# Half of the pair products of a feature-interaction kernel with the batch on the partitions

## The chip, the cores and the metric

The kernel runs on one core of a Trainium2 chip. The metric is the device time of one execution in microseconds, lower is better. On the core, TensorE multiplies matrices into PSUM, VectorE and ScalarE work on elements, GpSimd here only issues gathers, and SyncE only issues loads.

## The reference

A recommendation model's top: 32 embedding tables are looked up for a batch of 1,024, every pair of the 32 fields gets a bilinear form with a 64 x 64 matrix of its own, and three dense layers follow. All is fp32.

```python
iu, ju = jnp.triu_indices(32, k=1)                       # 496 pairs
p, q = e[:, iu, :], e[:, ju, :]                          # e: 1024 x 32 x 64, gathered
z = jnp.einsum('bpe,fpe,bpf->bp', p, kernel, q)          # kernel: 64 x 496 x 64
h = jnp.concatenate([z, dense_ctx], axis=1)              # 1024 x 512
h = jnp.maximum(h @ W_top1 + b_top1, 0.0)                # 512 -> 512
h = jnp.maximum(h @ W_top2 + b_top2, 0.0)                # 512 -> 256
y = h @ W_top3                                           # 256 -> 1
```

## The kernel before

The batch is cut into four quarters of 256 (`QB`). Two fields of 64 features make a **pack** of 128 partitions, so a quarter has 16 packs. GpSimd gathers the rows of a pack with four indirect DMAs into `raw`, batch on the partitions (L173). TensorE transposes the pack into the PSUM bank `prep_ps` (L307), and ScalarE copies it to `xt`, features on the partitions (L192). SyncE loads the pair matrices of pack k into `k_sb` (L161).

The pairs of pack k with the packs m below it are done in **units** (`UNITS`, L23) of up to two m each, 64 units in a quarter. For a unit TensorE multiplies the stationary pair matrices `k_sb` with the moving `xt` of pack m, four matmuls of 64 x 128 by 256 columns (L289 and L290, on the two halves of the array at a time), into one slot of `t_ps`. A unit with a single m (`len(ms) == 1`) uses the free quarter of the slot for the pairs inside the packs (L295, L297). `t_ps` has three slots (`TRING`), taken in the order of `TURNS`; before a slot is taken again TensorE waits for `prod_done`, the multiply that read it (`take_turn`, L268). VectorE multiplies the slot by `xt` of pack k into `prod` (L252; a single-m unit takes three instructions, L256, L258, L260). Now the 64 products of a pair lie on partitions, and TensorE sums them: a matmul with the stationary 0/1 matrix `sel_sb` of 32 columns adds the partitions into a row of `z_ps` (L321, L324), four such matmuls at a time on the four column groups.

The order is written out by hand. Four units make a **burst**. In burst b TensorE transforms the four units, then runs a piece of the layers of the quarter before, where one is due, then transposes packs that the next burst needs, then sums the products of burst b - 1 (L366 to L377). The layers have four **pieces** per quarter (L333), each of which takes a slot of `t_ps` in turn: two of 16 instructions with `w1_sb` (L343), one with `w2_sb` (L352), and one of four (L358). ScalarE copies `z_ps` to `zt` (L199) and applies the layers' bias and ReLU (L209, L212). Every fp32 matmul is two instructions in the trace.

Of the kernel before, what the change touches and what calls it, by code (L numbers as in the profile page):

```python
# [11 lines left out]
PACKS = FIELDS // 2  # L12
W = 2 * QB
ZT = 2
RAW = 16
XRING = 2 * PACKS
TRING = 3
PRING = 8
BURST = 4

UNITS = [(k, tuple(range(m, min(m + 2, k)))) for k in range(1, PACKS) for m in range(0, k, 2)]  # L23
NU = len(UNITS)
NB = NU // BURST
TILE_BURSTS = NB // ZT
PACK_COL = [P * (k * (k - 1) // 2) + EMBED * (k // 2) for k in range(PACKS + 1)]
KCOLS = PACK_COL[PACKS]


def weight_cols(k, m):

    begin = PACK_COL[k] + P * m
    return slice(begin, begin + (EMBED if m == k else P))


def burst_sums(b):

    sums = [(u, n) for u in range(b * BURST, (b + 1) * BURST) for n in range(2)]
    return sorted(sums, key=lambda un: un[1] == 1 and len(UNITS[un[0]][1]) == 1)  # L40

Z_SLOT = {un: (b // TILE_BURSTS, at % 4, 2 * (b % TILE_BURSTS) + at // 4)
          for b in range(NB) for at, un in enumerate(burst_sums(b))}

FREE = [Z_SLOT[u, 1] for u, (_, ms) in enumerate(UNITS) if len(ms) == 1]
FREE_GROUPS = sorted({(t, g) for t, g, _ in FREE})


def packs_due(b):

    q, at = divmod(b, NB)
    if q >= QUARTERS:
        return []
    last = UNITS[at * BURST + BURST - 1][0]
    due = [k for k in range(PACKS) if k <= last and (at == 0 or k > UNITS[at * BURST - 1][0])]
    if at == 0 and q:
        due = due[2:]
    due = [q * PACKS + k for k in due]  # L60
    if at == NB - 1 and q < QUARTERS - 1:
        due += [(q + 1) * PACKS, (q + 1) * PACKS + 1]
    return due


def before_sums(b):


    return packs_due(b)[:1] if b > NB else []


def after_sums(b):
    return packs_due(b)[len(before_sums(b)):]

PIECES = 4
PIECE_BURST = 2
# [4 lines left out]
def piece_after(b):  # L83

    q, at = divmod(b, NB)
    return (q - 1, at - PIECE_BURST) if q and 0 <= at - PIECE_BURST < PIECES else None

# [5 lines left out]

def turns():

    out = []
    for b in range(QUARTERS * NB):
        out += [("unit", b * BURST + n) for n in range(BURST)]
        if piece_after(b):
            out.append(("piece", piece_after(b)))  # L100
    return out + [("piece", (QUARTERS - 1, piece)) for piece in range(PIECES)]

# [5 lines left out]
def build(nc, ids, tables, kmat, dense, w1, b1, w2, b2, w3, sel, sel_dense, ident, y):  # L108
    fp32, i32 = mybir.dt.float32, mybir.dt.int32
    ALU, ACT = mybir.AluOpType, mybir.ActivationFunctionType  # L110
    ctx = ExitStack()
    with ctx:
# [9 lines left out]
        sel_dense_sb = sb("sel_dense_sb", [P, len(FREE_GROUPS), 32])  # L122
        w1_sb = sb("w1_sb", [P, 2 * ZT, H1])
# [4 lines left out]
        dense_sb = sb("dense_sb", [P, BATCH])  # L128
        k_sb = sb("k_sb", [P, KCOLS])
        raw = sb("raw", [P, RAW, BT, 2, EMBED])  # L130
        xt = sb("xt", [P, XRING, QB])
        prod = sb("prod", [P, PRING, 4, QB])
        zt = sb("zt", [P, ZT, W])
        h1 = sb("h1", [P, H1 // P, QB])
        h2 = sb("h2", [P, H2 // P, QB])
        y_sb = sb("y_sb", [1, BATCH])

        t_ps = ctx.enter_context(nc.psum_tensor("t_ps", [P, TRING, 4, QB], fp32))
        prep_ps = ctx.enter_context(nc.psum_tensor("prep_ps", [P, QB], fp32))
# [309 lines left out]
```

## Time and profile before

| | us |
|---|---|
| median of 3 runs | 472.48 |
| lowest, highest | 471.53, 472.54 |
| the profiled execution | 471.08 |
| span of its profile | 469.3 |
| TensorE busy (share of the span) | 438.2 (93%) |
| VectorE busy | 305.6 (65%) |
| GpSimd busy | 241.9 (52%) |
| ScalarE busy | 42.0 (9%) |
| mean granted TensorE clock | 0.996 |

The busy time of an engine is the union of its instructions' records. Matmuls overlap in the array, so the mean duration of one is longer than the distance from one to the next. The granted clock is at its full level in nearly every stretch. "Idle before" names what an engine waited for. The chain of work that ended last follows each wait back to what ended it.

### The profile page before, as it was taken

The page shows a single profiled execution, that of the slowest core. Times are in us where ns is not written, and L with a number is a line of the kernel's source. Part 1 is how long each engine was busy: PE and PEld are TensorE (multiplying, and loading weights), DVE is VectorE, ACT ScalarE, POOL GpSimd, SP SyncE. Part 2 cuts the span into 40 slices and gives each one's busy share as a digit, 9 for nine tenths or more (in the row PEclk, how much of TensorE's full clock was granted, in tenths as well). Part 3 has the DMA queues.
Part 4 walks back from the last instruction along what each step waited for, and adds up shares of the span by engine and source line. Part 5 has one row for each costly group of instructions (what it writes and reads, how often), then busy time and mean ns, then how long its engine had stood idle before and what let it go on. Part 6 is the DMA issues. An engine that isn't in the chain of part 4 may idle for free.

```text
span 469.3 us, 7916 instructions
## 1 busy us (share of the span) xinstructions
PE 438.2 (93%) x3432; PEld 263.1 (56%) x3432; DVE 305.6 (65%) x320; ACT 42.0 (9%) x101; POOL 241.9 (52%) x260
## 2 busy tenths in 40 slices
PE   0159999999999999999999999999999999999988
PEld 0036556556456765665556674565556765565646
DVE  0045878788774656788777456788787437878850
ACT  1000000100111110000011110000001110000002
POOL 5777777777777777777777777753300000000000
PEclk9998999999999999999999999999999999999999
DMA  4444454511111111111111111110000000000000
GB/s 125 110 114 135 134 168 154 162 28 27 27 27 28 27 27 29 27 26 30 27 30 25 27 29 27 27 22 13 11 3 0 1 1 0 1 1 1 0 1 0
DMA packets 11834, 19.41 MB, mean 41 GB/s; under 512 B 5141, under 2 KB 5785, under 8 KB 11673
## 3 DMA queue, kind: packets, MB, share of 16 engines
q0 software_dynamic: 8192, 8.40, 10.1%
q1 hardware_dynamic: 2592, 8.34, 5.6%
q10 hardware_dynamic: 1016, 2.17, 1.3%
q8 instruction: 27, 0.44, 0.4%
q14 instruction: 7, 0.05, 0.0%
HBM read 18.89 MB, written 0.00 MB: 40 GB/s over the span
## 4 chain that ended last, share of the span: by engine, by line
PE 91%; POOL 5%; issue 2%; DMA 1%; DVE 1%; ACT 0%; DVEq 0%
PE t_ps L289 46%; PE z_ps L321 23%; PE t_ps L343 6%; POOL raw L173 5%; PE prep_ps L307 4%; PE t_ps L295 3%; PE t_ps L352 3%; PE t_ps L290 1%; PE z_ps L324 1%; PE t_ps L358 1%; DVE prod L252 1%; DMA raw<-tbl,ids_sb 1%; PE z_ps L329 1%; DMA ids_sb<-ids 1%; ACT xt L192 0%
## 5 line engine op out<-in xcount | busy, mean ns | idle before, releaser
L252 DVE TENSOR_TENSOR prod<-t_ps,xt 128x1024 f32<-128x1024 f32 x224 | 259.1, 1215 | 93.1 <-PE t_ps L290 93.1
L173 POOL DMA_INDIRECT raw<-tbl,ids_sb x256 | 241.7, 944 | 93.7 <-issue 76.2
L289 PE MATMUL t_ps<-xt,k_sb 64*128 64x256 f32 x960 | 232.4, 390 | 0.0
L290 PE MATMUL t_ps<-xt,k_sb 64*128 64x256 f32 x960 | 232.4, 390 | 0.0
L289 PEld LDWEIGHTS t_ps<-xt,k_sb 64*128 64x128 f32 x960 | 172.3, 188 | 67.7 <-issue 26.6
L290 PEld LDWEIGHTS t_ps<-xt,k_sb 64*128 64x128 f32 x960 | 172.4, 189 | 0.0
L321 PE MATMUL z_ps<-prod,sel_sb 128*32 128x512 f32 x960 | 122.9, 599 | 0.5 <-DVE prod L260 0.5
L321 PEld LDWEIGHTS z_ps<-prod,sel_sb 128*32 128x32 f32 x960 | 26.3, 109 | 54.7 <-issue 46.5
L256 DVE TENSOR_TENSOR prod<-t_ps,xt 128x512 f32<-128x512 f32 x32 | 21.9, 685 | 53.2 <-PE t_ps L297 53.2
L307 PE MATMUL prep_ps<-ident_sb,raw 128*128 128x128 f32 x128 | 28.5, 305 | 27.8 <-DMA raw<-tbl,ids_sb 26.7
L192 ACT ACTIVATE xt<-prep_ps 128x256 f32<-128x256 f32 x64 | 24.5, 382 | 284.6 <-PE prep_ps L307 283.3
L307 PEld LDWEIGHTS prep_ps<-ident_sb,raw 128*128 128x128 f32 x128 | 13.9, 144 | 55.1 <-issue 35.9
L343 PE MATMUL t_ps<-zt,w_sb 128*128 128x256 f32 x128 | 29.5, 385 | 0.8 <-ACT zt L199 0.8
L343 PEld LDWEIGHTS t_ps<-zt,w_sb 128*128 128x128 f32 x128 | 23.8, 190 | 6.6 <-DVE prod L252 2.4
L295 PE MATMUL t_ps<-xt,k_sb 64*64 64x256 f32 x64 | 21.1, 410 | 0.0
L297 PE MATMUL t_ps<-xt,k_sb 64*64 64x256 f32 x64 | 21.0, 410 | 0.0
L324 PE MATMUL z_ps<-prod,sel_sb 128*32 128x256 f32 x64 | 16.7, 379 | 0.0
L352 PE MATMUL t_ps<-h,w_sb 128*128 128x256 f32 x64 | 14.8, 384 | 0.0
L258 DVE TENSOR_TENSOR prod<-t_ps,xt 64x256 f32<-64x256 f32 x32 | 13.7, 427 | 0.4
L260 DVE TENSOR_TENSOR prod<-t_ps,xt 64x256 f32<-64x256 f32 x32 | 13.3, 417 | 0.4
L352 PEld LDWEIGHTS t_ps<-h,w_sb 128*128 128x128 f32 x64 | 11.9, 190 | 2.6 <-DVE prod L252 1.1
L209 ACT ACTIVATE h<-t_ps,b_sb 128x256 f32<-128x256 f32 x16 | 7.6, 473 | 57.2 <-PE t_ps L343 57.2
(15 smaller groups left out, 42.0 us busy)
## 6 DMA issues: line engine op xcount, KB each, us to landing
raw<-tbl,ids_sb POOLq DMA_INDIRECT x256, 2.5
w_sb<-w ACTq DMA_DIRECT2D x1, 1024.0 KB
k_sb<-kmat SPq DMA_DIRECT2D x1, 992.0 KB, 5.0
k_sb<-kmat SPq DMA_DIRECT2D x1, 896.0 KB
k_sb<-kmat SPq DMA_DIRECT2D x1, 864.0 KB, 4.5
k_sb<-kmat SPq DMA_DIRECT2D x1, 768.0 KB, 4.2
k_sb<-kmat SPq DMA_DIRECT2D x1, 736.0 KB, 4.0
k_sb<-kmat SPq DMA_DIRECT2D x1, 640.0 KB, 3.9
```

The lines of the kernel that those rows point to most:

```text
L173: nc.gpsimd.indirect_dma_start(raw[:, p % RAW, t, f, :], None, tables[2 * k + f], bass.IndirectOffsetOnAxis(ap=ids_sb[:, q * BT + t, 2 * k ...
L192: nc.scalar.activation(xt[:, p % XRING, :], prep_ps[:], ACT.Copy).then_inc(x_copied, 1)
L252: nc.vector.tensor_tensor(prod[:, own], t_ps[:, slot], xt[:, here:here + 1, :].broadcast_to([P, 4, QB]), ALU.mult).then_inc(prod_done, 1)
L256: nc.vector.tensor_tensor(prod[:, own, 0:4:2, :], t_ps[:, slot, 0:4:2, :], xt[:, here:here + 1, :].broadcast_to([P, 2, QB]), ALU.mult)
L289: nc.tensor.matmul(t_ps[:, slot, i, :], k_sb[0:EMBED, cols], xt[0:EMBED, x, :], start=True, stop=True)
L290: last = nc.tensor.matmul(t_ps[:, slot, 2 + i, :], k_sb[EMBED:P, cols], xt[EMBED:P, x, :], start=True, stop=True)
L295: nc.tensor.matmul(t_ps[EMBED:P, slot, 1, :], k_sb[0:EMBED, cols], xt[0:EMBED, xa, :], start=True, stop=True)
L307: last = nc.tensor.transpose(prep_ps[:, t * P:(t + 1) * P], raw[:, p % RAW, t, :, :], ident_sb[:])
L321: last = nc.tensor.matmul(z_ps[rows, :], weights, prod[:, own, 2 * n:2 * n + 2, :], start=(pos == 0), stop=(pos == 15 and (tile, group) no ...
L324: last = nc.tensor.matmul(z_ps[rows, 0:QB], weights, prod[:, own, 2, :], start=False, stop=False)
L343: last = nc.tensor.matmul(t_ps[:, slot, 2 * n, :], w1_sb[:, t, m * P:(m + 1) * P], zt[:, t // 2, t % 2 * QB:(t % 2 + 1) * QB], start=(t == ...
L352: last = nc.tensor.matmul(t_ps[:, slot, 2 * n, :], w2_sb[:, t, n * P:(n + 1) * P], h1[:, t, :], start=(t == 0), stop=(t == H1 // P - 1))
```

## The change

Half of the work changes its layout. For 16 blocks in a quarter (`BATCH_GROUPS`: pack k of 4 to 15 with the packs 0 to 3, and pack k of 12 to 15 also with the packs 4 to 7), the stationary operand is now `xt` of pack k for 128 samples, and the pair matrices `k_sb` move, 512 columns a matmul. The result in `t_ps` has the batch on the partitions. VectorE multiplies it by `raw`, the gathered rows themselves, into `prod_a` or `prod_d`, and the 64 products of a pair are now neighbours on one partition. Of these **batch units**, 32 in a quarter and 128 in all, VectorE sums every third and the last six itself with one reduction each (47), and ScalarE the other 81, each with 16 activations of 64 elements that also write their sum to `zb`. The other 32 units of a quarter, the **feature units**, stay as they were, column sums on TensorE included; their sums fill one `z_ps` bank per quarter instead of two.

A **round** now has four feature units and the four batch units of the round before, alternating (`order()`); there are 8 rounds in a quarter. The column sums come once per round. `t_ps` keeps its three slots. Once per quarter TensorE transposes `zb` (`turn_sums`), and ScalarE copies it to `zbt`, which feeds half of the first layer. Packs are transposed and copied in pairs of 512 columns. `raw` and `xt` have 24 slots (`SLOTS`); a gather into a slot that batch units read waits for the last batch unit of that quarter.

The core of the diff; what is left out are the constants' arithmetic, the placing of weights on the host, and the names of columns.

```diff
+GROUP = 4
+GF = 2 * GROUP
 W = 2 * QB
-RAW = 16
-XRING = 2 * PACKS
+SLOTS = 24
 TRING = 3
-PRING = 8
+FRING = 8
+ARING = 6
+DRING = 2
+BATCH_GROUPS = {k: (() if k < GROUP else (0,) if k < 3 * GROUP else (0, 1)) for k in range(PACKS)}
+F_UNITS = [(k, tuple(range(m, min(m + 2, k)))) for k in range(1, PACKS)
+           for m in range(0, k, 2) if m // GROUP not in BATCH_GROUPS[k]]
+B_UNITS = [(k, j, t) for k in range(PACKS) for j in BATCH_GROUPS[k] for t in range(BT)]
...
+def order():
+    out = []
+    for r in range(LAST + 1):
+        q, at = divmod(r, ROUNDS)
+        feature = [("F", q, at * BURST + n) for n in range(BURST)] if r < LAST else []
+        q, at = divmod(r - 1, ROUNDS)
+        batch = [("B", q, at * BURST + n) for n in range(BURST)] if r else []
+        mixed = [x for n in range(BURST) for x in feature[n:n + 1] + batch[n:n + 1]]
+        out.append(mixed)
+    return out
...
+def on_vector(q, u):
+    n = q * NBU + u
+    return n % 3 == 0 or n >= QUARTERS * NBU - 6
...
 # GpSimd
-                if p >= RAW:
-                    pool.wait_ge(transposed, p - RAW + 1)
+                if p >= SLOTS:
+                    before_q, before_k = divmod(p - SLOTS, PACKS)
+                    pool.wait_ge(prep_done, pair_copied(before_q, before_k))
+                    if before_k < 2 * GROUP:
+                        pool.wait_ge(prod_done, COUNT["B", before_q, NBU - 1])
...
 # ScalarE
+            def sum_along(q, u):
+                own = SCALAR_UNITS.index((q, u)) % ARING
+                act.wait_ge(prod_done, COUNT["B", q, u])
...
+                for n in range(2):
+                    for f in range(GF):
+                        last = nc.scalar.activation(prod_a[:, own, n, f, :], prod_a[:, own, n, f, :], ACT.Copy,
+                                                    accum_out=zb[:, q % 2, t, col + n * GF + f:col + n * GF + f + 1])
+                last.then_inc(reduced_a, 1)
...
+            for r in range(LAST + 1):
+                if piece_after(r):
+                    copy_layer(*piece_after(r))
+                if turned_after(r) is not None:
+                    copy_turned(turned_after(r))
+                for j in before_sums(r + 1):
+                    copy_pair(j)
+                if r and r % ROUNDS == 0:
+                    copy_z(r // ROUNDS - 1)
+                for j in after_sums(r + 1):
+                    copy_pair(j)
...
+                for kind, q, u in ORDER[r]:
+                    if kind == "B" and not on_vector(q, u):
+                        sum_along(q, u)
...
 # VectorE
+            def batch_multiply(q, u):
...
+                dve.wait_ge(t_done, COUNT["B", q, u])
+                nc.vector.tensor_tensor(
+                    out.rearrange("p n (g c) f -> p n g (c f)", g=GROUP),
+                    t_ps[:, slot].rearrange("p (n h) (g w) -> p n (h g) w", n=2, w=2 * EMBED),
+                    raw[:, first:first + GROUP, t, :].unsqueeze(1).broadcast_to([P, 2, GROUP, 2 * EMBED]),
+                    ALU.mult).then_inc(prod_done, 1)
+            def sum_along(q, u):
...
+                nc.vector.tensor_reduce(zb[:, q % 2, t, col:col + 2 * GF],
+                                        prod_d[:, n % DRING].rearrange("p n c f -> p (n c) f"),
+                                        AX.X, ALU.add).then_inc(reduced_d, 1)
...
 # TensorE
+            def batch_transform(q, u):
+                k, j, t = B_UNITS[u]
+                slot = take_turn(TURN_OF["B", q, u])
...
+                nc.tensor.matmul(t_ps[:, slot, 0:2, :], xt[0:EMBED, x, t * P:(t + 1) * P], k_sb[0:EMBED, cols],
+                                 start=True, stop=True)
+                nc.tensor.matmul(t_ps[:, slot, 2:4, :], xt[EMBED:P, x, t * P:(t + 1) * P], k_sb[EMBED:P, cols],
+                                 start=True, stop=True).then_inc(t_done, 1)
...
+            def turn_sums(q):
+                pe.wait_ge(prep_copied, PREP_COUNT["turn", q] - 1)
+                pe.wait_ge(reduced_a, sum(x[0] <= q for x in SCALAR_UNITS))
+                pe.wait_ge(reduced_d, sum(x[0] <= q for x in VECTOR_UNITS))
+                for c in range(2):
+                    for t in range(BT):
+                        at = c * QB + t * P
+                        last = nc.tensor.transpose(prep_ps[:, at:at + P], zb[:, q % 2, t, c * P:(c + 1) * P], ident_sb[:])
+                last.then_inc(prep_done, 1)
```

On TensorE, around the sums of a burst in the first quarter, the kernel before has sums (L321, L324), a transpose of one pack (L307) and then unit after unit, each with its wait for a slot (`prod_done`):

```order
L321 MATMUL z_ps<-prod,sel_sb 32x512 [waits z_copied,prod_done]
L321 MATMUL z_ps<-prod,sel_sb 32x512 x6
L324 MATMUL z_ps<-prod,sel_sb 32x256
L307 MATMUL prep_ps<-ident_sb,raw 128x128 [waits x_copied,gathered13]
L307 MATMUL prep_ps<-ident_sb,raw 128x128
L289 MATMUL t_ps<-xt,k_sb 128x256 [waits prod_done]
L290 MATMUL t_ps<-xt,k_sb 128x256
L289 MATMUL t_ps<-xt,k_sb 128x256
L290 MATMUL t_ps<-xt,k_sb 128x256
```

In the changed kernel, in the second quarter, a batch unit (L455, L457) follows every feature unit, and a pair of packs (L469) is transposed between two blocks of units, where `gathered` and `prep_copied` are waited for:

```order
L455 MATMUL t_ps<-k_sb,xt 128x512 [waits prep_copied,prod_done]
L457 MATMUL t_ps<-k_sb,xt 128x512
L469 MATMUL prep_ps<-ident_sb,raw 128x128 [waits gathered0,prep_copied]
L469 MATMUL prep_ps<-ident_sb,raw 128x128
L469 MATMUL prep_ps<-ident_sb,raw 128x128 [waits gathered1]
L469 MATMUL prep_ps<-ident_sb,raw 128x128
L493 MATMUL z_ps<-prod,sel_sb 32x512 [waits z_copied,prod_done]
L493 MATMUL z_ps<-prod,sel_sb 32x512 x5
L496 MATMUL z_ps<-prod,sel_sb 32x256 x2
L437 MATMUL t_ps<-xt,k_sb 128x256 [waits prep_copied,prod_done]
L438 MATMUL t_ps<-xt,k_sb 128x256
```

Between two blocks of sums there are now eight units, each with a wait for a slot, instead of four.

On VectorE the kernel before has only the multiplies, here a stretch with one single-m unit:

```order
L252 TENSOR_TENSOR prod<-t_ps,xt 128x1024 [waits t_done,summed,x_copied]
L252 TENSOR_TENSOR prod<-t_ps,xt 128x1024 [waits t_done]
L252 TENSOR_TENSOR prod<-t_ps,xt 128x1024 [waits t_done,x_copied]
L252 TENSOR_TENSOR prod<-t_ps,xt 128x1024 [waits t_done]
L256 TENSOR_TENSOR prod<-t_ps,xt 128x2x256 [waits t_done,summed]
```

The changed one alternates feature (L359, L363) and batch multiplies (L385), with a reduction (L399) one unit behind every third batch unit:

```order
L385 TENSOR_TENSOR prod_a<-t_ps,raw 128x1024 [waits t_done,reduced_a]
L359 TENSOR_TENSOR prod<-t_ps,xt 128x1024 [waits t_done,prep_copied]
L385 TENSOR_TENSOR prod_d<-t_ps,raw 128x1024 [waits t_done,reduced_d]
L359 TENSOR_TENSOR prod<-t_ps,xt 128x1024 [waits t_done,prep_copied]
L399 TENSOR_REDUCE zb<-prod_d 128x16 [waits prod_done]
L385 TENSOR_TENSOR prod_a<-t_ps,raw 128x1024 [waits t_done,reduced_a]
L359 TENSOR_TENSOR prod<-t_ps,xt 128x1024 [waits t_done,summed,prep_copied]
```

The reductions stand in the one queue that also frees the slots of `t_ps`.

On ScalarE the copies of the packs and of the layers stood alone before; now the sums of a round's batch units stand between one round's copies and the next round's, as here in the second quarter:

```order
L270 ACTIVATE xt<-prep_ps 128x512 [waits prod_done,prep_done]
L296 ACTIVATE prod_a,zb<-prod_a 128x64 [waits prod_done]
L296 ACTIVATE prod_a,zb<-prod_a 128x64 x15
L296 ACTIVATE prod_a,zb<-prod_a 128x64 [waits prod_done]
L296 ACTIVATE prod_a,zb<-prod_a 128x64 x15
L296 ACTIVATE prod_a,zb<-prod_a 128x64 [waits prod_done]
L296 ACTIVATE prod_a,zb<-prod_a 128x64 x15
L311 ACTIVATE h<-t_ps,b_sb 128x256 [waits layer_done] x2
L270 ACTIVATE xt<-prep_ps 128x512 [waits prod_done,prep_done]
```

A copy that is due while such sums run waits for them, since the queue is in order.

## Rows read from the trace of the kernel before

**Rows 1.** The page: busy us (share) xinstructions, and the chain that ended last

```profile
PE 438.2 (93%) x3432; PEld 263.1 (56%) x3432; DVE 305.6 (65%) x320; ACT 42.0 (9%) x101; POOL 241.9 (52%) x260
...
PE 91%; POOL 5%; issue 2%; DMA 1%; DVE 1%; ACT 0%; DVEq 0%
```

**Rows 2.** The page's costliest groups: busy us, mean ns | idle before, releaser

```profile
L252 DVE TENSOR_TENSOR prod<-t_ps,xt 128x1024 f32<-128x1024 f32 x224 | 259.1, 1215 | 93.1 <-PE t_ps L290 93.1
...
L307 PEld LDWEIGHTS prep_ps<-ident_sb,raw 128*128 128x128 f32 x128 | 13.9, 144 | 55.1 <-issue 35.9
```

**Rows 3.** The timeline of TensorE, 300 to 316 us: start us, us, what

```profile
301.01 0.44 PE L307 MATMUL prep_ps<-ident_sb,raw 128*128 128x128 f32 x2
301.38 1.92 PE L321 MATMUL z_ps<-prod,sel_sb 128*32 128x512 f32 x16
303.13 0.60 PE L329 MATMUL z_ps<-dense_sb,sel_dense_sb 128*32 128x256 f32 x4
303.66 0.48 PE L289 MATMUL t_ps<-xt,k_sb 64*128 64x256 f32 x1
...
304.20 0.38 PE L289 MATMUL t_ps<-xt,k_sb 64*128 64x256 f32 x1
...
304.42 0.38 PE L289 MATMUL t_ps<-xt,k_sb 64*128 64x256 f32 x1
...
309.53 0.48 PE L289 MATMUL t_ps<-xt,k_sb 64*128 64x256 f32 x1
```

**Rows 4.** The timeline of VectorE in the same stretch

```profile
301.86 0.68 DVE L256 TENSOR_TENSOR prod<-t_ps,xt 128x512 f32<-128x512 f32 x1
302.56 0.43 DVE L258 TENSOR_TENSOR prod<-t_ps,xt 64x256 f32<-64x256 f32 x1
303.00 0.42 DVE L260 TENSOR_TENSOR prod<-t_ps,xt 64x256 f32<-64x256 f32 x1
304.94 4.62 DVE L252 TENSOR_TENSOR prod<-t_ps,xt 128x1024 f32<-128x1024 f32 x4 [1.53 <-PE t_ps L290]
310.79 4.62 DVE L252 TENSOR_TENSOR prod<-t_ps,xt 128x1024 f32<-128x1024 f32 x4 [1.23 <-PE t_ps L290]
```

**Rows 5.** The chain in order of time: start us, us, what; quarters and pieces

```profile
128.75 0.41 PE t_ps L289
...
194.96 0.43 PE z_ps L329 x4
...
253.89 3.72 PE t_ps L343 x16
...
263.48 3.65 PE t_ps L343 x16
...
303.30 0.43 PE z_ps L329 x4
```

**Rows 6.** The timeline of the start: transposes of packs 2 and 3, a gather, the first unit

```profile
19.61 0.69 PE L307 MATMUL prep_ps<-ident_sb,raw 128*128 128x128 f32 x2 [4.20 <-DMA raw<-tbl,ids_sb]
...
24.72 0.94 POOL L173 DMA_INDIRECT raw<-tbl,ids_sb  x1 [0.30 <-issue]
...
24.80 0.69 PE L307 MATMUL prep_ps<-ident_sb,raw 128*128 128x128 f32 x2 [4.51 <-DMA raw<-tbl,ids_sb]
25.42 0.28 PEld L289 LDWEIGHTS t_ps<-xt,k_sb 64*128 64x128 f32 x1 [0.33 <-issue]
```

**Rows 7.** The timeline of the end: the first layer of the last quarter

```profile
455.58 7.15 PE L343 MATMUL t_ps<-zt,w_sb 128*128 128x256 f32 x32 [0.82 <-ACT zt L199]
```

**Rows 8.** The groups of ScalarE's copies, shapes kept apart

```profile
L192 ACT ACTIVATE xt<-prep_ps 128x256 f32<-128x256 f32 x64 | 24.5, 382 | 284.6 <-PE prep_ps L307 283.3 <-ACT y_sb L215 1.3
...
L199 ACT ACTIVATE zt<-z_ps 128x512 f32<-128x512 f32 x8 | 4.8, 597 | 36.6 <-PE z_ps L329 36.6
```

More of the change, by code:

```diff
@@ L37, in burst_sums @@
[L37 to L54, printed above, removed]
-        return []
[L56 to L63, printed above, removed]
@@ new lines, with pairs_due @@
+ORDER = order()
+COUNT = {unit: n + 1 for n, unit in enumerate(x for units in ORDER for x in units)}
+QUARTER_DONE = [max(COUNT["F", q, NF - 1], COUNT["B", q, NBU - 1]) for q in range(QUARTERS)]
+def on_vector(q, u):
+    n = q * NBU + u
+    return n % 3 == 0 or n >= QUARTERS * NBU - 6
+VECTOR_UNITS = [(q, u) for q in range(QUARTERS) for u in range(NBU) if on_vector(q, u)]
+SCALAR_UNITS = [(q, u) for q in range(QUARTERS) for u in range(NBU) if not on_vector(q, u)]
+def pairs_due(r):
+    q, at = divmod(r, ROUNDS)
+    if r >= LAST:
+        return []
+    last = F_UNITS[at * BURST + BURST - 1][0] // 2
+    first = F_UNITS[at * BURST - 1][0] // 2 + 1 if at else 0
+    return [q * PACKS // 2 + j for j in range(first, last + 1)]
@@ L94, in turns @@
+PREP_COUNT = {use: n + 1 for n, use in enumerate(prep_uses())}
 def turns():
     out = []
[L97 to L101, printed above, removed]
+    for r, units in enumerate(ORDER):
+        out += units
+        if piece_after(r):
+            out.append(("piece",) + piece_after(r))
+    return out + [("piece", QUARTERS - 1, piece) for piece in range(PIECES)]
@@ L156, in _ @@
             for k in range(1, PACKS):
[L157 to L159 removed]
+                if k >= GROUP:
+                    sp.wait_ge(prep_done, PREP_COUNT["pair", (k - GROUP) // 2])
                 cols = slice(PACK_COL[k], PACK_COL[k + 1])
@@ L320, in feature_sums @@
-                    if n == 0 or len(UNITS[u][1]) == 2:
+                    own = u % FRING
+                    if n == 0 or len(F_UNITS[u][1]) == 2:
                         last = nc.tensor.matmul(z_ps[rows, :], weights, prod[:, own, 2 * n:2 * n + 2, :],
-                                                start=(pos == 0), stop=(pos == 15 and (tile, group) not in FREE_GROUPS))
+                                                start=(pos == 0), stop=(pos == 15 and group not in FREE_GROUPS))
                     else:
-                        last = nc.tensor.matmul(z_ps[rows, 0:QB], weights, prod[:, own, 2, :],
-                                                start=False, stop=False)
@@ L326, in feature_sums @@
-                if at % TILE_BURSTS == TILE_BURSTS - 1:
-                    for n, (tile, group) in enumerate(FREE_GROUPS):
-                        if tile == at // TILE_BURSTS:
-                            last = nc.tensor.matmul(z_ps[32 * group:32 * group + 32, QB:W], sel_dense_sb[:, n, :],
-                                                    dense_sb[:, q * QB:(q + 1) * QB], start=False, stop=True)
+                        last = nc.tensor.matmul(z_ps[rows, 0:QB], weights, prod[:, own, 2, :], start=False, stop=False)
@@ L331, in feature_sums @@
+                if at == ROUNDS - 1:
+                    for n, group in enumerate(FREE_GROUPS):
+                        last = nc.tensor.matmul(z_ps[32 * group:32 * group + 32, QB:W], sel_dense_sb[:, q, n, :],
+                                                dense_sb[:], start=False, stop=True)
                 last.then_inc(summed, 1)
             def layer(q, piece):
-                slot = take_turn(TURN_OF["piece", (q, piece)])
+                slot = take_turn(TURN_OF["piece", q, piece])
```

352 lines of the change are left out of this document (218 added, 134 removed).

## The prediction

> **What bounds the kernel now.** I read the page's busy times and chain first. TensorE is on 91% of the chain that ended last and VectorE on 1% [rows 1]: almost everything between start and end is TensorE's instruction stream. Then the groups of instructions: VectorE's big multiply ran 224 times and was idle 93.1 us before it, every time for a matmul into `t_ps` [rows 2]; VectorE waits for TensorE, not the other way round. Then the timeline of one burst, to see what the stream consists of. A pair of matmuls on the two halves of the array starts every 0.215 us, a unit is four such pairs, 0.86 us; a full burst is 303.66 to 309.53 [rows 3]. Sixteen sum instructions take 1.75 us (301.38 to 303.13), two transposes 0.37, and each change of tile shape about 0.1. VectorE needs 4.62 us for four full units, 1.135 each when queued ((4.62 - 1.215) / 3), and then idles 1.2 to 1.5 us [rows 4]. So in a burst of 5.5 to 5.9 us VectorE has only about 1.2 us of air. That small air is what the change must live from.
>
> **What it removes.** Half of the units lose their two column-sum matmuls. Sums happen once per round of eight units, 32 times instead of 64. One such block costs TensorE 1.75 + 0.1 to enter it and 0.2 to leave it, about 2.1 us: 32 x 2.1 = 67 us less TensorE work. The transforms do not get cheaper: a batch unit moves 2 x 512 columns where a feature unit moves 4 x 256, in the same pairs, 0.86 us by [rows 3]. Four transposes per quarter are added, 0.65 + 0.1 us, 3 us in all. On TensorE's work alone the kernel would fall to about 405.
>
> **What it adds.** VectorE keeps one multiplication per unit (the batch one reads 1,024 elements of PSUM and writes 1,024; I take 1.135, the row it is nearest to) and gets 47 reductions. No reduction is in the trace. It reads 1,024 elements of a partition: an upper bound is a lone 1.215 us, a lower one 0.68, the 512-element row [rows 2, 4]; I take 1.135, since it reads as many elements as the multiply. VectorE: 305.6 + 47 x 1.135 = 359 us. ScalarE gets 81 units of 16 activations, 1,296 of them, each with an accumulator output.
>
> **Why the freed time does not reach the end.** `t_ps` still has three slots, so TensorE's unit n waits for VectorE's unit n - 3. In a burst of four units that never bites. In a round of eight it does. Take a round from TensorE's first unit at 0. VectorE starts 1.28 later (303.66 to 304.94) [rows 3, 4]. TensorE's eighth unit needs VectorE's fifth done: five multiplies 5.68, plus on average two thirds of a reduction 0.76, plus 0.43 for each `len(ms) == 1` unit (0.70 + 0.44 + 0.43 against 1.135, [rows 4]), 0.32 on average, plus 0.13 for the end of the record and the semaphore: 8.17. Its own 0.86 makes 9.03. Then four transposes (0.37 for two, 0.14 for each more, the time of its weight load: 0.65) [rows 2, 3], 0.1, the sums 1.75, 0.1: a plain round is 11.6 us. The bursts it replaces take 2 x 5.5 to 5.9. A piece of the layers adds 3.7 (a burst with one lasts 263.48 - 253.89 = 9.6, without 5.9 [rows 5]) and waits for the sixth unit's slot, 0.6: 15.9. A quarter is three such, one with the short last piece 13.4, one with the turned sums 12.4, three plain, and 1.4 for the second of two pairs that wait for the one `prep_ps` bank: 109.7 us. Before, a quarter is 303.30 - 194.96 = 108.3 [rows 5]. The steady state gains nothing: what the sums gave back is spent waiting for slots. With half as many rounds, the sums, transposes and pieces form stretches of 2.6 to 6.9 us in which VectorE is fed from at most three slots.
>
> **Start.** Packs land every 5.0 us (19.61, 24.80) [rows 6]. The old kernel works from 25.4 on one pack at a time, and its second quarter begins at 128.75 [rows 5, 6]. In the new one TensorE does round 0 (four units) and then, in its own order, transposes packs 4 to 7 before anything of round 1, so round 1 begins when pack 7 has landed and is copied: 24.8 + 4 x 5.0 + 1.2 = 46. Seven rounds of 11.6 and two waits for a copy put round 8, the second quarter, at 129: only half a microsecond later, because in the old kernel, too, the first quarter goes by what GpSimd gathers. Gathers of later quarters now wait for the last batch unit of the quarter before; GpSimd needs 1.25 us each [rows 6], 10 us for the eight of a pair of packs, and a round is 11.6, so they stay just hidden.
>
> **End.** The last four batch units have no feature unit beside them and their sums lie on VectorE: 1.28 + four multiplies and five reductions, 10.2, then transposes and copy 1.4, then the layers, 455.58 to 469.3 = 13.7 [rows 7]: 26.6 us from the start of the last round. Sum with ScalarE free: 129 + 3 x 109.7 + 26.6 = 485, that is +16 on the span of 469.3, of which 4 are the quarters' and 11 the end's (128.75 + 3 x 108.3 leaves the old one 15.6).
>
> **ScalarE.** Let a be what one accumulating activation takes when queued. Rows give 0.382 us for 256 columns and 0.597 for 512 [rows 8]: 0.84 ns a column and 0.167 fixed, so 0.221 for 64. The program that is built has a second ScalarE instruction behind each of them, which writes the accumulator. Low end: both overlap by the 0.08 that VectorE's rows show (1.215 against 1.135) and the second costs one fixed part: 0.221 + 0.167 - 0.16 = 0.23; were the second free, 0.14. High end: no overlap, 0.39. ScalarE is in program order: copy of the pair, then the two or three batch units of the round, then the next copy, for which TensorE waits. Three units need 48a + 0.9. At a = 0.23 that is 11.9, a few tenths more than a plain round; at 0.28 it is 14.3, 2.7 late, in some 13 plain rounds of three units, 35 us, of which the rounds without a due pair (about a third) hide their part: +24 us. I take 0.28: an instruction without a tensor to read should cost less than a whole fixed part, but ScalarE need not overlap as VectorE does. Beyond 0.31 ScalarE sets the time: 47 until its first unit, 1,296a, 37 of its other work, 13 of waits at 32 copies, 20 at the end: 0.33 gives 545, 0.39 gives 622.
>
> The Trainium skill's page "ScalarE: Activation LUTs", section "What ACT_TABLE_LOAD costs", gives 186 ns + 0.833 ns a column with 93 ns of overlap: an estimate of 0.15 us for 64 columns, accumulator not counted; by it ScalarE would never be late and the sum would stay 485. It agrees with the trace's 0.382 within 17 ns for a lone one; the overlap no row here shows. The skill's page "VectorE: DVE Perf Modes", section "The TRN2 errata", speaks against this change: an SBUF source costs ScalarE 224 cycles fixed against 172 from PSUM, paid per instruction, and it advises tiles of 512 elements or more. By it 64 columns are an estimate of 0.24 us before any accumulator read, and the sum rises to 490 or more. No run here shows an SBUF source on ScalarE.
>
> **Rivals.** (1) ScalarE keeps up (a at most 0.24): 485 to 495. For it: 0.23 is a bound from rows. (2) ScalarE becomes the bound (a above 0.31): 530 to 600. For it: nothing in the trace shows ScalarE instructions overlapping. (3) Faster: slots do not hold TensorE. That needs the batch multiply and the reduction clearly under the 1.135 row; then VectorE keeps ahead, and the time is 469.3 - 67 + 3 + 16 of start and end = 421. The two rows of VectorE at 1,024 and 512 elements scale with elements, which speaks against it; it breaks even only if both cost about 1.0 us. (4) The middle case, my forecast: ScalarE late in the rounds with three units, 497 to 528.
>
> **How the numbers follow.** Span 485 + 24 = 509; the profiled execution took 471.08 with a span of 469.3, so 1.8 lies outside, and the median of the runs is 1.4 above it: 512. Chances: forecast 0.40, keeps up 0.28, ScalarE the bound 0.21, faster 0.09, no difference 0.02. Range: 484, the foot of rival 1, to 585, which is a = 0.36; a tenth stays below, a tenth above. A measurement of this kernel tells about 0.2% from no change, so faster 0.09, same 0.02, slower 0.89.
>
> **What would show it.** In the profile after: busy TensorE near 380 us with idle time before `t_ps` matmuls whose releaser is VectorE or a ScalarE copy (right), or TensorE still above 90% of the chain (rival 3). First sums at 55 to 56 us. Sums of column type every 11.6 us in rounds without pieces and 15 to 16 with them. The activation of L296 with its accumulator instruction: 16 of them per unit in 3.7 us is rival 1, 4.5 the forecast, over 5 rival 2, and then ScalarE leads the chain. Reduction near 1.2 us; a batch multiply longer than 1.3 would add to every round. The prediction is wrong if rounds are shorter than 11 us while `t_ps` has three slots.

## The result, and the profile after

The changed kernel takes 494.68 us (median of 4 runs, 493.90 to 495.66) where the kernel before takes 472.0: a ratio of 1.0485, 95% interval 1.0455 to 1.0516. Slower, inside the range, and 17 us under the predicted 512. It is the case that the prediction called rival 1, ScalarE keeps up (485 to 495). The profiled execution took 494.39 with a span of 492.6.

The page after, busy times and chain, answers to [rows 1]:

```profile
PE 409.6 (83%) x2416; PEld 196.9 (40%) x2416; DVE 355.8 (72%) x367; ACT 346.4 (70%) x2661; POOL 241.9 (49%) x260
...
PE 38%; issue 20%; DVE 19%; ACT 10%; POOL 9%; DMA 2%; DVEq 0%; ACTq 0%; POOLq 0%
```

TensorE fell from 91% of the chain to 38%, VectorE rose from 1% to 19%. Most of "issue" is VectorE too: of the chain's 98.5 us under that name, 73 stand right before an instruction of VectorE, for instance between its back-to-back instructions from 285.9 to 290.5 us. Together that is a third of the span. No engine is over 83% busy: the time is now made of engines that wait for each other. The page's groups (line, engine, operation, busy us, mean ns, idle before them) say what the new instructions cost, beside [rows 2]:

```profile
L296 ACT ACTIVATE prod_a<-prod_a 128x64 f32<-128x64 f32 x1296 | 309.4, 243 | 2.2 <-ACT y_sb L317 1.2
L296 ACT ACTIVATION_READ_ACCUMULATOR prod_a<-prod_a 128x1 f32 x1296 | 245.3, 189 | 0.0
...
L359 DVE TENSOR_TENSOR prod<-t_ps,xt 128x1024 f32<-128x1024 f32 x96 | 116.3, 1212 | 41.2 <-PE t_ps L438 39.5
...
L385 DVE TENSOR_TENSOR prod_a<-t_ps,raw 128x1024 f32<-128x1024 f32 x81 | 97.9, 1209 | 0.0
...
L399 DVE TENSOR_REDUCE zb<-prod_d 128x16 f32<-128x1024 f32 x47 | 56.5, 1204 | 0.0
```

The batch multiply (1.209) and the reduction (1.204) cost what the old multiply did (1.215). Who waits for whom is in the waits (us in total, times, longest); lines 437 and 455 are the first transforms of a feature and a batch unit, 385 the batch multiply:

```profile
PEld t_ps L437 <- DVE prod_a L385: 61.3, 48, 2.0
...
PEld t_ps L455 <- DVE prod L359: 24.6, 63, 0.4
PE t_ps L437 <- DVE prod_a L385: 23.0, 21, 1.1
...
PEld t_ps L437 <- DVE prod_d L385: 17.6, 22, 0.8
```

These waits for a slot of `t_ps` take the place of TensorE's unbroken stream. (The matrix part and the weight part of one wait are listed apart and overlap, so they are not to be added.) A round with a piece of the layers shows both sides. First TensorE, 286 to 298 us, where a number in brackets is its idle time and what ended it; then VectorE there:

```profile
290.54 0.48 PE L437 MATMUL t_ps<-xt,k_sb 64*128 64x256 f32 x1 [1.13 <-DVE prod_a L385]
...
292.80 1.13 PE L515 MATMUL t_ps<-zt,w_sb 128*128 128x256 f32 x4
...
296.45 1.93 PE L493 MATMUL z_ps<-prod,sel_sb 128*32 128x512 f32 x16
```

```profile
292.67 1.21 DVE L359 TENSOR_TENSOR prod<-t_ps,xt 128x1024 f32<-128x1024 f32 x1
293.80 1.21 DVE L385 TENSOR_TENSOR prod_d<-t_ps,raw 128x1024 f32<-128x1024 f32 x1
299.59 1.22 DVE L359 TENSOR_TENSOR prod<-t_ps,xt 128x1024 f32<-128x1024 f32 x1 [4.58 <-PE t_ps L438]
```

Within the units TensorE waits for VectorE (1.13). Then come piece and sums in one stretch, TensorE feeds nobody, and VectorE stands for 4.58 us. It stood as long behind the old kernel's pieces, in that kernel's timeline of VectorE:

```profile
260.89 3.49 DVE L252 TENSOR_TENSOR prod<-t_ps,xt 128x1024 f32<-128x1024 f32 x3 [4.80 <-PE t_ps L290]
...
270.41 4.62 DVE L252 TENSOR_TENSOR prod<-t_ps,xt 128x1024 f32<-128x1024 f32 x4 [4.56 <-PE t_ps L290]
```

But there TensorE did not wait for it afterwards; here it is needed for five units in a row before TensorE's eighth. With three slots neither engine can work ahead over the other's stretch.

A quarter ends with the matmul of the dense features; its starts give a clock for the four quarters (ns min/median/max, first and last start):

```profile
L499 PE MATMUL z_ps<-dense_sb,sel_dense_sb x4: 379/379/379, 142.0 to 142.7; 128*32 128x256 f32 x4
```

Read the same way in every kernel, the same matmul gives this table (us; the last column is what follows the fourth up to the span's end):

| kernel | 1st quarter | 2nd | 3rd | 4th | end | span |
|---|---|---|---|---|---|---|
| before | 134.6 | 108.4 | 108.3 | 102.9 | 15.1 | 469.3 |
| after | 142.0 | 112.9 | 109.5 | 103.9 | 24.3 | 492.6 |

Of the 23.3 us of span, 7.4 are in the first quarter, 6.7 in the others and 9.2 in the end. The last batch units stand before the fourth of these matmuls, so "end" is the last reductions and the layers alone.

### The profile page after: what moved, and what is told of

Its sections match the earlier page's. It is cut to its first block, busy times and chain, and to the rows that moved or that the text cites. A ratio compares the mean times of both kernels' runs of the same rounds, so it can differ in the third digit from the quotient of the medians.

```text
span 492.6 us, 8787 instructions
## 1 busy us (share of the span) xinstructions
PE 409.6 (83%) x2416; PEld 196.9 (40%) x2416; DVE 355.8 (72%) x367; ACT 346.4 (70%) x2661; POOL 241.9 (49%) x260
## 3 DMA queue, kind: packets, MB, share of 16 engines
q1 hardware_dynamic: 2592, 8.42, 4.8%
## 4 chain that ended last, share of the span: by engine, by line
PE 38%; issue 20%; DVE 19%; ACT 10%; POOL 9%; DMA 2%; DVEq 0%; ACTq 0%; POOLq 0%
ACT prod_a L296 9%; POOL raw L250 9%; PE t_ps L437 9%; PE z_ps L493 8%; PE t_ps L515 6%; DVE prod_a L385 6%; PE t_ps L455 6%; DVE prod L359 4%; PE t_ps L523 3%; DVE zb L399 3%; PE prep_ps L469 2%; DMA raw<-tbl,ids_sb 2%; DVE prod_d L385 2%; PE t_ps L442 2%; DVE prod L363 2%
## 5 line engine op out<-in xcount | busy, mean ns | idle before, releaser
L296 ACT ACTIVATE prod_a<-prod_a 128x64 f32<-128x64 f32 x1296 | 309.4, 243 | 2.2 <-ACT y_sb L317 1.2
L296 ACT ACTIVATION_READ_ACCUMULATOR prod_a<-prod_a 128x1 f32 x1296 | 245.3, 189 | 0.0
L437 PE MATMUL t_ps<-xt,k_sb 64*128 64x256 f32 x448 | 129.2, 404 | 23.1 <-DVE prod_a L385 23.0
L359 DVE TENSOR_TENSOR prod<-t_ps,xt 128x1024 f32<-128x1024 f32 x96 | 116.3, 1212 | 41.2 <-PE t_ps L438 39.5
L455 PE MATMUL t_ps<-k_sb,xt 64*128 64x512 f32 x256 | 141.0, 632 | 0.6 <-issue 0.6
L457 PE MATMUL t_ps<-k_sb,xt 64*128 64x512 f32 x256 | 141.0, 632 | 0.0
L438 PE MATMUL t_ps<-xt,k_sb 64*128 64x256 f32 x448 | 129.2, 404 | 0.0
L437 PEld LDWEIGHTS t_ps<-xt,k_sb 64*128 64x128 f32 x448 | 77.9, 190 | 114.2 <-DVE prod_a L385 61.3
L385 DVE TENSOR_TENSOR prod_a<-t_ps,raw 128x1024 f32<-128x1024 f32 x81 | 97.9, 1209 | 0.0
L438 PEld LDWEIGHTS t_ps<-xt,k_sb 64*128 64x128 f32 x448 | 77.9, 190 | 0.0
L363 DVE TENSOR_TENSOR prod<-t_ps,xt 128x512 f32<-128x512 f32 x32 | 21.9, 684 | 77.0 <-PE t_ps L444 77.0
L493 PE MATMUL z_ps<-prod,sel_sb 128*32 128x512 f32 x448 | 64.2, 611 | 0.0
L469 PE MATMUL prep_ps<-ident_sb,raw 128*128 128x128 f32 x128 | 23.6, 300 | 46.0 <-DMA raw<-tbl,ids_sb 39.2
L385 DVE TENSOR_TENSOR prod_d<-t_ps,raw 128x1024 f32<-128x1024 f32 x47 | 56.8, 1210 | 0.5 <-PE t_ps L457 0.4
L399 DVE TENSOR_REDUCE zb<-prod_d 128x16 f32<-128x1024 f32 x47 | 56.5, 1204 | 0.0
L455 PEld LDWEIGHTS t_ps<-k_sb,xt 64*128 64x128 f32 x256 | 39.7, 186 | 40.2 <-DVE prod L359 24.6
L469 PEld LDWEIGHTS prep_ps<-ident_sb,raw 128*128 128x128 f32 x128 | 14.3, 146 | 63.9 <-issue 32.7
L457 PEld LDWEIGHTS t_ps<-k_sb,xt 64*128 64x128 f32 x256 | 39.7, 186 | 0.0
L493 PEld LDWEIGHTS z_ps<-prod,sel_sb 128*32 128x32 f32 x448 | 13.9, 110 | 30.9 <-issue 26.6
```

Source lines behind the costliest of these rows:

```text
L296: last = nc.scalar.activation(prod_a[:, own, n, f, :], prod_a[:, own, n, f, :], ACT.Copy, accum_out=zb[:, q % 2, t, col + n * GF + f:col + ...
L359: nc.vector.tensor_tensor(prod[:, own], t_ps[:, slot], xt[:, here:here + 1, :].broadcast_to([P, 4, QB]), ALU.mult).then_inc(prod_done, 1)
L363: nc.vector.tensor_tensor(prod[:, own, 0:4:2, :], t_ps[:, slot, 0:4:2, :], xt[:, here:here + 1, :].broadcast_to([P, 2, QB]), ALU.mult)
L385: nc.vector.tensor_tensor(out.rearrange("p n (g c) f -> p n g (c f)", g=GROUP), t_ps[:, slot].rearrange("p (n h) (g w) -> p n (h g) w", n= ...
L399: nc.vector.tensor_reduce(zb[:, q % 2, t, col:col + 2 * GF], prod_d[:, n % DRING].rearrange("p n c f -> p (n c) f"), AX.X, ALU.add).then_i ...
L437: nc.tensor.matmul(t_ps[:, slot, i, :], k_sb[0:EMBED, cols], xt[0:EMBED, x, :], start=True, stop=True)
```

## Experiments

Two theories stood after the result. SLOTS: VectorE's reductions and the long rounds cost, through the turn of three slots, and ScalarE only shadows them. SCALAR: ScalarE's 1,296 accumulating activations cost, and TensorE waits for the copies queued behind them. The diffs below are against the changed kernel; "..." marks what is left out.

**x_scalar: without ScalarE's sums.**

```diff
-                for n in range(2):
-                    for f in range(GF):
-                        last = nc.scalar.activation(prod_a[:, own, n, f, :], prod_a[:, own, n, f, :], ACT.Copy,
-                                                    accum_out=zb[...])
+                last = nc.scalar.activation(zb[:, q % 2, t, col:col + 2 * GF],
+                                            prod_a[:, own, :, :, 0:1].rearrange("p n c f -> p (n c f)"), ACT.Copy)
```

> Leaves out ScalarE's sums: each of its 81 batch units gets one copy of one feature per pair instead of 16 accumulating activations, so ScalarE is never late. Theory SLOTS (rounds of eight units against three slots of t_ps set the time, ScalarE adds little): the whole order followed with the measured durations gives a span of 487, so 489 us, 5 to 6 below the changed kernel's 494.7. Rival SCALAR (the copies that stand behind ScalarE's sums are what made the change slower; ScalarE has 9% of the chain): at least 20 us less, 475 or below. Pure TensorE work would give 420 to 440.

Measured: 491.53 us (490.76 to 491.75, clear of the changed kernel's 493.90 to 495.66), ratio to before 1.0418 [1.0389, 1.0446], span 489.9; SLOTS expected 489. ScalarE fell from 346.4 us busy to 49.3 and the span by 2.7:

```profile
PE 409.6 (84%) x2416; PEld 197.2 (40%) x2416; DVE 355.7 (73%) x367; ACT 49.3 (10%) x150; POOL 241.9 (49%) x260
...
PE 44%; issue 22%; DVE 21%; POOL 9%; DMA 2%; ACT 1%; DVEq 0%; POOLq 0%
```

SCALAR is out for this kernel, although 10% of the changed kernel's chain stood at ScalarE: with that gone, TensorE has 44% of the chain instead of 38, VectorE 21 instead of 19, and the time hardly moves.

**x_vector: VectorE's reduction reads one feature of 64.**

```diff
-                                        prod_d[:, n % DRING].rearrange("p n c f -> p (n c) f"),
+                                        prod_d[:, n % DRING, :, :, 0:1].rearrange("p n c f -> p (n c) f"),
```

> Leaves out VectorE's sums: each of the 47 reductions reads one of the 64 features, 16 elements a partition, so VectorE loses 47 x about 1.05 = 50 us of work and keeps the instructions. SLOTS: only reductions that stand ahead of a unit whose slot TensorE waits for count, and the four at the end count in full: span 464, so 466 us, 28 below. A plain sum of VectorE's work would give 445, since then all 50 us come off. SCALAR: nothing to gain but the end, 488 or more.

Measured: 465.74 us, 0.986 [0.9813, 0.9907], span 464.8. The reduction now holds VectorE for 0.09 us (201.87 to 201.96 in its timeline):

```profile
201.87 0.17 DVE L399 TENSOR_REDUCE zb<-prod_d 128x16 f32<-128x16 f32 x1
201.96 1.22 DVE L385 TENSOR_TENSOR prod_a<-t_ps,raw 128x1024 f32<-128x1024 f32 x1
```

47 x 1.04 = 49 us less VectorE work is 27.8 us less span, and the 466 that SLOTS expected. The prediction's way of counting gives nearly this: two thirds of a reduction in front of the slot that the eighth unit needs, 0.76 in each of 31 rounds, is 23.6, and five reductions at the end are 5.7, 29.3 in all (the table below has 20.6 in the quarters and 7.2 in the end). SLOTS holds, and the reductions alone are more than the whole loss of 23.3.

**x_slots2: two slots instead of three.**

```diff
-TRING = 3
+TRING = 2
```

> TRING = 2: t_ps has two slots instead of three, nothing else changes. SLOTS: TensorE's unit n now waits for VectorE's unit n - 2, so one more unit of VectorE, 1.13 us, stands in each of the 32 rounds: span 532, so 534 us, about 40 above. SCALAR: ScalarE is not touched, and the time stays within 5 us of 494.7.

Measured: 542.33 us, 1.1495 [1.1464, 1.1527], span 541.4. One slot less costs 49 us, 8 more than SLOTS expected, with the same instructions on every engine. Where the 8 come from stays open.

**x_slower2: does the forecast's sum give 512 when its assumption is true?** Three more accumulating activations in each ScalarE unit make 19 x 0.239 = 4.54 us of it, as if one took 0.284, the forecast's value.

```diff
-ARING = 6
+ARING = 5
+EXTRA = 3
...
+                for n in range(EXTRA):
+                    nc.scalar.activation(spare[:, own, n, 0:EMBED], ident_sb[:, 0:EMBED], ACT.Copy,
+                                         accum_out=spare[:, own, n, EMBED:])
```

> The kernel of the run x_slower again, on such a chip: three more accumulating activations in each of ScalarE's units, 4.54 us a unit instead of 3.82, as if one took 0.284 us, the duration that the forecast of 512 was made with. The forecast's own sum gives 510 to 516; if ScalarE is far from the path (3 us, as the run without its sums shows, being all it ever costs) at most 500; if each wait of ScalarE costs more than the sum says, over 525.

Measured: 518.64 us, 1.1024 [1.0972, 1.1076], span 516.2. The chain in order of time shows ScalarE's units back to back, 3.82 us of the unit's own and the next 4.53 later:

```profile
112.24 3.82 ACT prod_a L301 x32
...
116.77 3.82 ACT prod_a L301 x32
...
121.31 3.82 ACT prod_a L301 x32
```

That is 23.6 us of span over the changed kernel and 26.3 over the one without ScalarE's sums, where the prediction put 24 for 0.28; the time lies 3 us above the 510 to 516 expected. The mechanism of the forecast is real, and it begins somewhere between 0.239 and 0.284: 19% more ScalarE work turned a cost of 3 us into 26. Only the total is as the forecast counted it, though. Against x_scalar the last round starts 27.5 us later, and 23.5 of that come in five rounds, 3.0 to 5.8 each, where the forecast had some thirteen rounds of 2.7 with a third hidden; that both sums meet is in part luck. The run has a ring of five product tiles instead of six; no run tells what that does alone.

**x_cadence: rounds of four units.** Sums and transposes come in stretches half as long, sums twice as often, the pieces are three short rounds apart, each batch unit stands two short rounds behind, and the first four feature units change their order.

```diff
+F_UNITS[:4] = [F_UNITS[n] for n in (1, 2, 0, 3)]
...
-BURST = 4
+BURST = 2
...
-        q, at = divmod(r - 1, ROUNDS)
+        q, at = divmod(r - 2, ROUNDS)
...
-TURN_ROUND, PIECE_ROUND = 2, 3
+TURN_ROUND, PIECE_ROUNDS = 3, (4, 7, 10, 13)
...
-                if r >= 2 and u % BURST == 0:
+                if r >= 4 and u % BURST == 0:
...
-                    dve.wait_ge(summed, r - 1)
+                    dve.wait_ge(summed, r - 3)
```

> The same units and the same work in rounds of four (two feature and two batch units) instead of eight, as the old bursts were: a block of sums comes after every four units with four matmuls instead of after eight with eight; the pieces of the layers are three rounds apart, and packs are transposed as soon as the shorter rounds ask for them. SLOTS: stretches without a unit are half as long and VectorE is fed through them: span 471, so 473 us, 22 below the changed kernel, level with the old one. SCALAR: ScalarE's work is the same and its order as well, so 485 or more.

Measured: 480.53 us, 1.018 [1.0146, 1.0214], span 478.9: 14 us gained of the 22 expected. The short blocks of sums take back some of it: a unit starts 1.00 us after the start of a block of eight matmuls, and 1.85 after one of sixteen in the changed kernel, so two short blocks cost 0.15 more than a long one, 32 times, 5 us.

```profile
299.52 1.07 PE L496 MATMUL z_ps<-prod,sel_sb 128*32 128x512 f32 x8
300.52 0.48 PE L440 MATMUL t_ps<-xt,k_sb 64*128 64x256 f32 x1
```

The table below says where the 14 lie: 11.6 in the first quarter and 9.6 in the second, while the third and fourth quarters and the end are 3.6, 2.2 and 1.7 longer than the changed kernel's. Short rounds alone are no gain everywhere.

**best2: short rounds, one round of lag, reductions placed anew.** VectorE reduces units 1, 4, 7, ... of each quarter and the last three instead of the last six; a batch unit stands one short round behind.

```diff
+LAG = 1
...
-        q, at = divmod(r - 1, ROUNDS)
+        q, at = divmod(r - LAG, ROUNDS)
...
-    return n % 3 == 0 or n >= QUARTERS * NBU - 6
+    return (n % NBU) % 3 == 1 or n >= QUARTERS * NBU - 3
...
-TURN_ROUND, PIECE_ROUND = 2, 3
+TURN_ROUND, PIECE_ROUNDS = 2, (3, 6, 9, 12)
```

> The kernel of the run best1 again, on a chip on which the kernel before takes its 472 us; there it took 599, and VectorE stood idle many times for 9 to 39 us with work at hand, so nothing of that comparison can be read. SLOTS (VectorE's reductions in the turn of three PSUM slots, and rounds of eight units with one unit's lag, make the loss) expects 455 to 459: 480.5 of the short rounds, less 10 to 14 for the batch units that come one short round earlier, less 10 to 12 for the place of the reductions. If the reductions' place and the lag do nothing, 478 to 482.

Measured: 453.55 us, 0.9612 [0.9574, 0.965], span 452.8, just under the 455 to 459 expected. It is faster than both kernels, with the same transforms, multiplies and sums as the changed one; only their order differs, and one unit more on ScalarE. Its page:

```profile
PE 401.5 (89%) x2416; PEld 200.5 (44%) x2416; DVE 355.4 (78%) x366; ACT 350.8 (77%) x2693; POOL 241.9 (53%) x260
```

and its largest waits for a slot, against 61.3 and 23.0 above:

```profile
PEld t_ps L448 <- DVE prod_a L396: 33.5, 44, 1.6
...
PE t_ps L448 <- DVE prod_a L396: 1.7, 3, 0.7
```

| kernel | 1st quarter | 2nd | 3rd | 4th | end | span |
|---|---|---|---|---|---|---|
| x_scalar | 140.3 | 111.9 | 108.2 | 103.9 | 25.6 | 489.9 |
| x_vector | 140.1 | 105.5 | 106.0 | 96.1 | 17.1 | 464.8 |
| x_slower2 | 153.1 | 118.3 | 113.3 | 107.1 | 24.4 | 516.2 |
| x_cadence | 130.4 | 103.3 | 113.1 | 106.1 | 26.0 | 478.9 |
| best2 | 133.6 | 99.7 | 101.3 | 93.9 | 24.3 | 452.8 |

**Inconclusive: what part of best2 did it.** Two kernels were to split the 27 us between x_cadence and best2 and to take both sums out together. In both comparisons that had them, on two chips, the kernel before took 594 to 599 us instead of 472, and every kernel beside it was slower as well: best2's kernel 742.37 us (the run best1), x_slower2's 793.64 (x_slower), and the two below 751.16 (x_lag) and 728.99 (x_both) the first time. One of the two chips had run the first four experiments undisturbed.

> The kernel of the run x_lag again, on such a chip: rounds of four units, the batch units one short round behind instead of two, VectorE's split as in the changed kernel. 480.5 with two rounds, 453.6 with one round and the reductions placed anew. SLOTS (both count, 10 to 14 each) expects 464 to 470; if the lag did it alone 453 to 457; if the place of the reductions did it alone 478 to 482.

Measured: 749.54 us, 1.2628 [1.2565, 1.269] to a before of 594.43. This is best2's order with the changed kernel's choice of VectorE's units.

> The kernel of the run x_both again, on a chip on which the kernel before takes its 472 us (there it took 599). Both sums left out: ScalarE copies one feature of each pair, VectorE's reduction reads one feature of 64. SLOTS expects 455 to 462: 466 of the run without VectorE's reductions, less 4 to 11 where ScalarE came next. Were ScalarE off the path once the reductions are gone, 464 to 467. The bound of TensorE and the two engines that it hands its slots to, without any sum, is what this run gives.

Measured: 727.64 us, 1.2246 [1.2183, 1.2308]. Nothing of these is compared with the other runs. The timeline of VectorE in best1, the disturbed run of best2's kernel, shows why:

```profile
81.62 0.69 DVE L374 TENSOR_TENSOR prod<-t_ps,xt 128x512 f32<-128x512 f32 x1 [32.38 <-remote]
```

VectorE stood still for 32.38 us and the trace names nobody of this kernel as the one it waited for; there are some fifteen such gaps in this run, of 7.8 to 36.7 us. They are not spread evenly. The page's busy tenths of VectorE and GpSimd, in 40 slices of the span, first best1, then best2:

```profile
DVE  0000001599975010168897302027889710788990
...
POOL 6777774000006777300000777720000177000000
```

```profile
DVE  0024899999949797979979797799969797799930
...
POOL 5777777777607777777017777776027771000000
```

In the 318 us in which best1 issues its gathers, VectorE is busy for 36 us; in the 318 us of best2's gathers it is busy for 260. The gathers themselves take GpSimd 241.9 us in both. So in the disturbed runs VectorE hardly works while gathers are issued. Why that is so in these two comparisons and not in the others stays open.

What part of the 27 us is the lag's and what the reductions' places' was not measured on its own, but the table allows a reading. A quarter has 32 batch units, no multiple of three, so x_cadence's choice of every third unit falls differently in each quarter, and in the second it is the choice of best2 (units 1, 4, 7, ...). There best2 gains 3.6, by the lag and the placing of the pieces that goes with it. In the third and fourth quarters, where the places differ as well, it gains 11.8 and 12.2. That speaks for the places as the larger part, and in the disturbed comparison x_lag and best1, which differ in the places alone, lie 8.8 us apart the same way; still it is an argument from one trace each, not a test. The end column shows little of the lag (1.7), because the last batch units stand before it: from the start of the last round best2 takes 26.7 us (426.14 to 452.8) and x_cadence 31.4 (447.48 to 478.9), 4.8 less for two batch units less, of the 5 to 6 expected there. In turn best2's first quarter is 3.2 us longer, as it holds two batch units more.

## Why the prediction was right, and where its sum was off

**What bounds the kernel, and what the change removes.** Right in kind: VectorE's 1.2 to 1.5 us of air in a burst was the budget, and the runs x_vector and x_slots2 show that it was overdrawn through the slots. The sign was decided there, and that part of the argument was no luck: without ScalarE's sums the prediction had a span of 485, and x_scalar has 489.9. The indicator "busy TensorE near 380" was off: it is 409.6. Most of that is probably not work: a first matmul after a wait is recorded 0.1 longer (0.48 against 0.38), and the record of the last one before it runs on for 0.17 in which a next could have begun (0.38 against the 0.215 between pairs); at some 130 waits for a slot that is 35 us.

**VectorE.** 359 us foreseen, 355.8 measured; a reduction at 1.204 us, near the upper bound of 1.215 and of the kind taken.

**The round.** Predicted 11.6 plain, 15.9 with a piece. Sums start at 281.13 and, behind the round of the fence above, at 296.45: 15.3. The piece follows its unit at once (292.80 in the fence), so the 0.6 that the prediction gave to its wait for a slot is not there. The plain rounds later in that quarter take 12.1, 12.2 and 11.7. Together, round 8 starts at 130.28 and the last round at 462.94, so three quarters take 332.7, 110.9 each against 109.7: 3.5 us short in all. In the run without ScalarE's sums they take 330.4, 1.3 over the predicted 329.1; the other 2.3 are ScalarE's.

**Start.** Round 1 was put at 46 (with 5.0 us a pack, where the two times of [rows 6] are 5.19 apart) and began at 45.43; the first sums at 55 to 56 and came at 56.88. In between, TensorE had waited for gathers and its granted clock was down (us, busy of PE, PEld, DVE, ACT, POOL, granted clock):

```profile
25.00:45.00 20.00, 8.42 (x41) 4.68 (x42) 5.33 (x8) 1.19 (x2) 15.12 (x17) 0.79 0.42 128
45.00:50.00 5.00, 5.00 (x18) 2.15 (x19) 1.78 (x4) 0.60 (x1) 3.78 (x5) 0.50 0.69 231
```

0.50 is the lower of its two levels, 1.2 GHz, right behind a stretch in which it was busy 8.42 of 20 us; the pairs there start 0.42 to 0.59 us apart instead of 0.215. Before, 25 to 50 us ran at 0.93. Still, round 8 began only 1.3 us late. (The 7.4 of the first table is mostly a longer round 8: the quarter's dense matmul stands behind eight units now, not four.) The gathers were called just hidden; from 130 to 460 us TensorE waited three times for one, 4.7 us in all.

**End.** 26.6 predicted, 462.94 to 492.6 = 29.7 measured. VectorE's timeline, then TensorE's:

```profile
472.95 2.33 DVE L399 TENSOR_REDUCE zb<-prod_d 128x16 f32<-128x1024 f32 x2
```

```profile
475.43 1.09 PE L479 MATMUL prep_ps<-ident_sb,zb 128*128 128x128 f32 x4 [6.09 <-DVE zb L399]
477.30 2.05 PE L515 MATMUL t_ps<-zt,w_sb 128*128 128x256 f32 x4 [0.78 <-ACT zbt L277]
479.14 1.67 PE L515 MATMUL t_ps<-zbt,w_sb 128*128 128x256 f32 x4
480.64 1.03 PE L515 MATMUL t_ps<-zt,w_sb 128*128 128x256 f32 x4
```

VectorE had one multiply of the round before left (1.13 of the 3.1), and behind 6.09 us of idling TensorE ran its first eight matmuls at about half speed (3.34 us from 477.30 to 480.64, the next four 0.86), so the layers took 15.3 against 13.7 in [rows 7]. An idle engine is paid for twice here. The run x_vector shows it from the other side: there TensorE idles 0.89 us at this point, the granted clock stays at its full level (1.00 from 448 to 455), the first eight take 1.80 us and the layers 13.8.

With these three terms the sum comes to the measured span: 485 + 1.3 + 3.5 + 3.1 = 492.9 beside 492.6. They hold ScalarE's share too. The ScalarE-free sum itself is to be laid beside x_scalar: round 8 at 128.5 (129 predicted), 330.4 for three quarters (329.1), 31.0 for the end (26.6), 489.9 in all. So it was 5 us short, nearly all of it in the end, and ScalarE adds 1.8 before round 8, 2.3 in the quarters and takes 1.4 off the end, 2.7 in all.

**ScalarE: the mis-sized term.** This is the step that made 512 of 495; that the result lies in the range all the same is owed to rival 1, with which the range begins. The prediction took 0.28 us for an accumulating activation between bounds of 0.23 and 0.39. ScalarE's timeline:

```profile
249.95 0.24 ACT L296 ACTIVATE prod_a<-prod_a 128x64 f32<-128x64 f32 x1
250.09 0.18 ACT L296 ACTIVATION_READ_ACCUMULATOR prod_a<-prod_a 128x1 f32 x1
250.18 0.24 ACT L296 ACTIVATE prod_a<-prod_a 128x64 f32<-128x64 f32 x1
```

One starts every 0.239 us: the accumulator's read of 0.19 lies half beside its own activation and half beside the next. 16 make 3.82 us, the 3.7 of rival 1 and not the 4.5 of the forecast. "ScalarE need not overlap as VectorE does" was the wrong reason; it overlaps more, 0.19 of the 0.43 that the two records last. Instead of +24 the term is worth +2.7 (x_scalar), and x_slower2 shows that at 0.284 it would have been worth 26.

Two statements of the Trainium skill were weighed ahead. By "VectorE: DVE Perf Modes", section "The TRN2 errata", a 64-column activation with its source in SBUF is an estimate of 0.24 us. The record of 0.243 agrees. By "ScalarE: Activation LUTs", section "What ACT_TABLE_LOAD costs", it is an estimate of 0.15 when queued, with no accumulator counted. At first sight the 0.239 from start to start speaks for the first statement, but x_scalar, where ScalarE reads SBUF without an accumulator, speaks for the second:

```profile
308.34 0.46 ACT L294 ACTIVATE zb<-prod_a 128x16 f32<-128x16 f32 x3
```

Each of these records lasts 0.221 us, so three in 0.46 start 0.12 apart and overlap by 0.10. By the first statement's figures one of 16 columns is an estimate of 0.20, by the second's of 0.11 when queued. With the 0.84 ns a column of [rows 8], 64 columns without an accumulator would start some 0.16 apart, an estimate from these rows, and the accumulator's read then costs about 0.08 of the 0.239. So ScalarE does overlap, and the forecast's bound of 0.23 came near for a reason close to its own: two fixed parts, less two overlaps. The times that went with the two statements, 490 or more and 485, both lie nearer to the span of 492.6 than the forecast's 509.

## What to carry to other kernels

Work taken from the engine that bounds the kernel comes back only if the slots between it and its partner let it run ahead: count, for the unit that needs the slot, what stands in front of it on the other engine, and do that for the longest stretch in which one of the two feeds nobody. When such a change disappoints, try another order before giving it up: short rounds alone gave 14 us, and with a shorter lag and the reductions spread evenly nearly the same instructions went from 4.9% slower to 3.9% faster. And where a cost has no row, the forecast should say what happens just above and just below it; here 0.239 us per activation cost 3 us in all and 0.284 cost 26.

## What the runs showed of the hardware that was not expected

- A 64-column activation in SBUF with an accumulator output is two records, 243 and 189 ns, and one starts every 239 ns: the two together hold the queue for less than the first record alone. Without the accumulator, activations of 16 columns from SBUF start 120 ns apart at records of 221.
- A reduction of 1,024 fp32 elements of a partition to 16 takes VectorE as long as a multiply that writes 1,024 (1,204 against 1,209 ns), and 0.17 us when it reads 16.
- TensorE's granted clock was at 1.2 GHz around and after gaps of 3.06 to 6.09 us: behind the waits for gathers at 41 and 45 us until 50 us, and behind the 6.09 at the end until 480.
- In two comparisons every kernel, the one before too, was 26 to 64% slower than in the others, and in the profiled ones VectorE's work had gaps that name no releaser within the kernel, most of them while GpSimd issued gathers (36 us of VectorE work in 318 us of gathers, against 260 in the same kernel undisturbed).
